# Pair 0's attention scores from fp32 row groups, with both first halves split and sent ahead, and row maxima taken for two tiles at a time

## The reference

```python
x_gate = g * jnp.tanh(jax.nn.softplus(g)); x = (x_gate * x_inner) @ W3_w.T + W3_b   # + position
h = jnp.concatenate([h, txt], axis=1)
q = (ln(h) @ Wq + bq)  # 8 heads, two halves of 16 each; k alike; v: 8 heads of 16
a1 = softmax(q1 @ k1.T * scale); a2 = softmax(q2 @ k2.T * scale)
h = h + (a1 - 0.5 * a2) @ v
h = h + experts(ln(h)) + shared(ln(h))
```

## Time and profile before

| | us |
|---|---|
| median of 3 runs | 237.06 (236.85 to 237.62) |
| the profiled execution, its own time | 235.49 |
| its span | 233.5 |
| TensorE busy | 189.9 (81%) |
| VectorE busy | 145.4 (62%) |
| ScalarE busy | 112.6 (48%) |
| GpSimd busy | 96.0 (41%) |
| first instruction of pass one of pair 0 | 33.0 |
| first instruction of pass two (start of the paired stage) | 54.2 |

### The profile page before, as it was taken

How to read it: one execution, slowest core, us unless ns; L and a number is a source line. 1 busy time by engine, 2 the same in 40 slices (tenths; PEclk the granted TensorE clock), 3 DMA queues, 4 the chain that set the end, 5 groups by cost and what they waited for, 6 DMA issues and landing times.

```text
span 233.5 us, 4897 instructions
## 1 busy us (share of the span) xinstructions
PE 189.9 (81%) x1615; PEld 135.6 (58%) x1615; DVE 145.4 (62%) x483; ACT 112.6 (48%) x213; POOL 96.0 (41%) x130
## 2 busy tenths in 40 slices
PE   0669278588988998896988999998989987999960
PEld 0538134134644554543644444468989986999950
DVE  4799779984596658798589754748333333455420
ACT  2125142033767666675477757631566645466310
POOL 4300418800882486010100006005777777777440
PEclk9999959555999999999799999999999999999996
DMA  5911986565637464859735597020444333331000
GB/s 189 297 27 50 102 152 101 110 105 102 120 91 144 98 119 57 156 103 255 253 101 179 192 273 102 0 68 3 124 103 104 87 85 80 72 64 40 25 12 0
DMA packets 20332, 25.35 MB, mean 109 GB/s; under 512 B 3393, under 2 KB 16199, under 8 KB 20308
## 3 DMA queue, kind: packets, MB, share of 16 engines
q1 hardware_dynamic: 17817, 20.68, 38.9%
q0 software_dynamic: 1888, 3.81, 7.1%
q10 hardware_dynamic: 603, 0.54, 1.6%
HBM read 12.17 MB, written 3.62 MB: 68 GB/s over the span
## 4 chain that ended last, share of the span: by engine, by line
PE 45%; DVE 19%; issue 10%; DMA 9%; POOL 6%; ACT 4%; SPq 2%; ACTq 1%; POOLq 0%; DVEq 0%
PE bank L1558 8%; PE bank L1360 7%; DVE smax L908 6%; PE bank L1313 6%; PE bank L1571 5%; PE bank L1342 4%; DMA stacks<-parts 4%; PE bank L1291 4%; POOL p_ring L556 3%; DMA p_ring<-hb_scratch,id_u 3%; PE bank L1374 3%; ACT p_ring L668 2%; PE bank L1400 2%; DMA stacks<-mx_p 2%; PE bank L1221 1%
## 5 line engine op out<-in xcount | busy, mean ns | idle before, releaser
L908 DVE TENSOR_REDUCE smax<-bank 128x2 f32<-128x384 f32 x96 | 51.2, 552 | 22.7 <-PE bank L1313 21.9
L668 ACT ACTIVATE p_ring<-bank 128x384 f32<-128x384 f32 x96 | 44.9, 494 | 31.4 <-PE bank L1342 29.9
L1313 PE MATMUL bank<-stacks 96*128 96x192 bf16 (+1 forms) x256 | 35.7, 273 | 10.3 <-DVE smax L908 5.1
L1342 PE MATMUL bank<-stacks 99*128 99x192 bf16 (+1 forms) x256 | 32.0, 253 | 3.2 <-ACT p_ring L668 2.6
L1313 PEld LDWEIGHTS bank<-stacks 96*128 96x128 bf16 (+1 forms) x256 | 15.6, 108 | 32.5 <-DVE smax L908 16.8
L1558 PE MATMUL bank<-p_ring,parts 128*128 128x128 f32 x208 | 27.2, 276 | 0.6 <-DVE p_ring L1160 0.6
L1558 PEld LDWEIGHTS bank<-p_ring,parts 128*128 128x128 f32 x208 | 25.3, 192 | 0.8 <-DVE p_ring L1160 0.8
L742 ACT ACTIVATE p_ring<-bank 128x512 f32<-128x512 f32 x19 | 11.4, 598 | 26.3 <-PE bank L1558 26.3
L573 POOL DMA_INDIRECT out_dram<-oT,out_u x19 | 19.0, 1000 | 10.9 <-DVE oT L1186 7.0
L1342 PEld LDWEIGHTS bank<-stacks 99*128 99x128 bf16 (+1 forms) x256 | 17.3, 107 | 8.3 <-ACT p_ring L668 5.5
L556 POOL DMA_INDIRECT p_ring<-hb_scratch,id_u x19 | 19.3, 1014 | 5.8 <-issue 5.2
(11 more groups left out here) (171 smaller groups left out, 319.4 us busy)
## 6 DMA issues: line engine op xcount, KB each, us to landing
stacks<-in_w_dram SPq DMA_DIRECT2D x12, 512.0 KB, 5.0
stacks<-parts SPq DMA_DIRECT2D x47, 96.0 KB, 3.6
stacks<-stacks SPq DMA_DIRECT2D x14, 192.0 KB, 3.1
stacks<-stacks SPq DMA_DIRECT2D x16, 96.0 KB, 3.5
wp_sb<-in_wpack_dram SPq DMA_DIRECT2D x1, 900.0 KB, 6.7
hb_scratch<-h SPq DMA_DIRECT2D x3, 256.0 KB, 3.0
stacks<-in_wn_dram SPq DMA_DIRECT2D x1, 512.0 KB, 4.4
hx_scratch<-hn SPq DMA_DIRECT2D x1, 387.0 KB
```

The costliest lines, as they stand in the source:

```text
L668: act.activation(p_ring[:, half % 2, TJ * (hd % 4) + ORDER[i], :, :], bank[2 + g % 2][:, 0:2 * SEQ].rearrange("p (s q) -> p s q", s=2), AC ...
L908: dve.tensor_reduce(smax[:, p % 2, j, 2 * hd:2 * hd + 2], bank[g % 2][:, 0:2 * SEQ].rearrange("p (s k) -> p s k", s=2), AX.X, ALU.max, neg ...
L1313: ins = pe.matmul(bank[g % 2][r0:r0 + rn, SEQ * s:SEQ * (s + 1)], q_st[p % NST][0:SROWS, 2 * hd + s, 128 * j + r0:128 * j + r0 + rn], k_st ...
L1342: ins = pe.matmul(bank[2 + g % 2][r0:r0 + rn, SEQ * s:SEQ * (s + 1)], k_st[p % NST][0:SROWS + NPART, 2 * hd + s, 128 * j + r0:128 * j + r0 ...
```

## The change

- Pair 0's pass one no longer uses the stacks. q and k are projected a second time with columns in another order (`rows`, L1347; weights laid out by GpSimd, eight operations), so that each group of 32 partitions holds two slots of 16. ScalarE writes them to `q_rows` and, twice, to `k_rows`, once with either slot of each group multiplied by zero (`evac_rows`). `score0(k)` then makes four matmuls in fp32, one for each group of 32 rows (eight for the middle tile), into the four banks `s_banks`. `row_max0(k)` takes four slots at once: 12 reductions of 768 columns for 24 of 384. There is one set of four banks, so `score0(k + 1)` waits for `row_max0(k)`.
- The parts of pairs 0 and 1: ScalarE makes f, hi and mid, GpSimd makes both differences (`rest`, `low`), none of it is on VectorE. The order (`TURNS0`) is first half of pair 0, first half of pair 1, second halves. Parts 4 to 7 lie in `p_ring`.
- SyncE sends in the new order below; from pair 2 on the parts of the second half's q go before the maximum and the copies of the first half. ScalarE issues no copies and no maximum any more.
- The gate matmuls of group 2 go before pair 0's turns; its gate function is shared by GpSimd (six operations) and VectorE (product and reciprocal). Pair 1's norm is made ahead of the first row maximum, that of tiles 6 to 11 between the maxima, and ScalarE normalises all six of these tiles in one go after it.

```diff
+        s_banks = ctx.enter_context(nc.psum_tensor("s_banks", [128, 4, 512], F32))
+        bank = [s_banks[:, i, :] for i in range(4)] + [ctx.enter_context(nc.psum_tensor(f"bank{i}", [128, 512], F32)) for i in range(4, 8)]
...
         GH = TJ * HEADS // 2
         p_ring = sb("p_ring", [128, 2, GH, 2, SEQ])
+        EARLY_Q = 2 * PT
+        EARLY_K = EARLY_Q + HS // 4 * PT
+        early = p_ring[:, 0, :, :, :].rearrange("p g s q -> p (g s q)")
+        q_rows = early[:, 0:EARLY_Q].rearrange("p (c t) -> p c t", c=2)
+        k_rows = early[:, EARLY_Q:EARLY_K].rearrange("p (u t) -> p u t", u=HS // 4)
+        wq_rows, wk_rows = [early[:, EARLY_K + 256 * m:EARLY_K + 256 * (m + 1)].rearrange("p (c n) -> p c n", c=2) for m in range(2)]
+        early_parts = p_ring[:, 1, :, :, :].rearrange("p g s q -> p (g s q)")[:, 0:4 * NPART * PT // 2].bitcast(BF16)\
...
+        ROWS0 = [("rows", c, m) for c in range(2) for m in range(2)]
+        misc_order = ROWS0[0:2] + proj_items(0)[0:2] + ROWS0[2:4] + proj_items(1)[0:2] + proj_items(0)[2:5] + proj_items(1)[2:4] + [("max", 0, 0), ("proj", 1, 4)]
...
                 if p >= NST:
                     sp.wait_ge(st_ready, TJ * HEADS * (p - NST + 1))
-                for m, st, order in ((0, q_st[b], Q_PARTS), (1, k_st[b], K_PARTS)):
+                todo = [(part, m) for m in ms for part in range(NPART)]
+                for part, m in sorted(todo) if p < 2 else todo:
+                    st, order = ((q_st[b], Q_PARTS), (k_st[b], K_PARTS))[m]
                     r = 4 * p + 2 * ch + m
-                    for part in range(NPART):
-                        j = order.index(part)
-                        if part < 2:
...
                     .then_inc(max_ld[p % NST][ch], 16)
-            for ch in range(2):
-                gather_parts(1, ch)
-                copy_blocks(1, ch)
+            gather_parts(0, 0)
+            gather_parts(1, 0)
+            copy_blocks(0, 0)
+            copy_blocks(1, 0)
+            gather_parts(0, 1)
+            load_max(0, 0)
+            gather_parts(1, 1)
+            copy_blocks(0, 1)
+            load_max(0, 1)
...
+            sp.wait_ge(h_mm, 3)
+            ones_rows(2)
             for p in range(2, PAIRS):
-                load_max(p - 2, 1)
                 gather_parts(p, 0)
+                gather_parts(p, 1, (0,))
+                if p == PAIRS - 1:
+                    gather_parts(p, 1, (1,))
...
+            def rest(k):
+                f = f_ring[:, k % NF, :]
+                pool.wait_ge(hi_act, k + 1)
+                pool.tensor_tensor(f, f, parts_of(TURNS0[k])[:, 0, :], ALU.subtract).then_inc(rest_done, 1)
+            def low(k):
+                pr = parts_of(TURNS0[k])
+                pool.wait_ge(rest_done, k + 1)
+                pool.wait_ge(mid_act, k + 1)
+                pool.tensor_tensor(pr[:, 2, :], f_ring[:, k % NF, :], pr[:, 1, :], ALU.subtract).then_inc(split_done[k % NF], 1)
...
+                    for l in range(2):
+                        pool.tensor_scalar(dst[:, :, l, :], src[:, :, l, :], by, 0.0, ALU.mult, ALU.add).then_inc(w_rows_done, 1)
+            last = GROUPS[2]
+            pool.wait_ge(ex_done, 3)
+            link(pool.tensor_scalar(gm[:, last], ex[:, last], 1.0, 2.0, ALU.mult, ALU.add))
+            link(pool.tensor_tensor(mu[:, last], gm[:, last], ex[:, last], ALU.mult))
+            link(pool.tensor_scalar(mu[:, last], mu[:, last], MISH_TOP, 0.0, ALU.min, ALU.add))
+            pool.tensor_scalar(mr[:, last], mu[:, last], 1.0, 2.0, ALU.mult, ALU.add).then_inc(mr_done, 1)
+            for k in range(2):
+                rest(k)
+            for k in range(2):
+                low(k)
+            pool.wait_ge(rec_done, 1)
+            link(pool.tensor_tensor(mu[:, last], mu[:, last], ex[:, last], ALU.mult))
+            pool.tensor_tensor(g_sb[:, last], mu[:, last], inner[:, last], ALU.mult).then_inc(act_done, 1)
+            pool.wait_ge(act_done, 3)
+            for k in range(2, ACT_SPLITS, 2):
+                rest(k)
+                rest(k + 1)
+                low(k)
+                low(k + 1)
+            pool.wait_ge(split_done[(ACT_SPLITS - 1) % NF], 2)
+            for r in range(ACT_SPLITS, 4 * PAIRS):
                 split(r)
...
+            def evac_rows(c, m, l=0):
+                item = ("rows", c, m)
+                act.wait_ge(misc_ready, misc_no[item] + 1)
+                src = mbank(item)[:, 0:PT]
+                if m == 0:
+                    act.activation(q_rows[:, c, :], src, ACT.Identity, bias=bqw4[:, c:c + 1]).then_inc(wide_done, 1)
+                else:
+                    act.activation(k_rows[:, 2 * c + l, :], src, ACT.Identity, bias=bkw[:, 2 * c + l:2 * c + l + 1], scale=rows_of[:, l:l + 1]).then_inc(wide_done, 1)
...
-            exp_gate(2)
-            copies_k0(True)
-            copies_k0(False)
+            act.wait_ge(bq_done, 3)
+            act.wait_ge(rows_done, 1)
+            def f_hi(k):
+                evac_proj(TURNS0[k] // 4, TURNS0[k] % 4)
+                hi(k)
+            evac_rows(0, 0)
+            evac_rows(0, 1, 0)
+            evac_rows(0, 1, 1)
+            f_hi(0)
+            f_hi(1)
+            mid(0)
+            evac_rows(1, 0)
+            mid(1)
+            evac_rows(1, 1, 0)
+            evac_rows(1, 1, 1)
             copy_hnT(1)
-            normalise(LN_TEXT, 1)
-            for n in range(4):
-                evac_proj(1, n)
+            f_hi(2)
+            f_hi(3)
+            mid(2)
+            mid(3)
+            f_hi(4)
+            f_hi(5)
...
+            def row_max0(k):
+                u, i = divmod(k, TJ)
+                dve.wait_ge(s_ready, 2 * (k + 1))
+                dve.tensor_reduce(smax[:, 0, ORDER[i], 4 * u:4 * u + 4], s_banks[:, :, 0:SEQ], AX.X, ALU.max, negate=True).then_inc(s_max, 2)
...
+            def pair1_norm():
+                n = image_tokens(1)
                 yield
                 dve.wait_ge(dve_step, n)
-                for t in LN_LAST:
-                    n = step(dve.bn_aggr(mv[:, t, :], stats[:, t, :]))
+                yield from stats_steps((4,))
+                yield from norm_steps(slice(TJ, 2 * TJ))
+                for t in LN_FIRST:
+                    yield ln_apply((t,))
+            def last_factor():
+                c = GROUPS[2]
+                dve.wait_ge(inner_done, 3)
+                n = step(dve.scalar_tensor_tensor(inner[:, c], tok_bank(2, 0), bn_[:, 0:1], inner[:, c], ALU.add, ALU.mult))
                 yield
                 dve.wait_ge(dve_step, n)
-                n = step(dve.tensor_scalar(ve[:, sl], mv[:, sl, 1], EPS, None, ALU.add))
+                dve.wait_ge(mr_done, 1)
+                yield dve.reciprocal(ex[:, c], mr[:, c]).then_inc(rec_done, 1)
...
-                    n = step(ins)
-                    yield
-                    dve.wait_ge(dve_step, n)
-                yield ln_bias(sl)
...
-                row_max(0, a // TJ, a % TJ)
-                next(splitting, None)
-                for _ in range((a >= 3) + (a >= GH + 4)):
+                yield from stats_steps((7, 10))
+                yield from norm_steps(slice(2 * TJ, T))
+                yield ln_bias(slice(2 * TJ, T))
+            for _ in pair1_norm():
+                pass
+            splitting, last_mish, rest_text, last_norm = iter(()), last_factor(), stats_steps((6, 8, 9, 11)), last_norm_steps()
+            for k in range(TJ * HEADS // 2):
+                row_max0(k)
+                if k == 0:
+                    for _ in last_mish:
+                        pass
+                for _ in range(4 if 1 <= k <= 2 else 0):
+                    next(rest_text, None)
+                if k == 3:
+                    for _ in rest_text:
+                        pass
+                if k == 6:
+                    take_v(0)
+                for _ in range(2):
...
+            def rows(c, m, tiles=range(TJ)):
+                item = ("rows", c, m)
+                if tiles[0] == 0:
+                    wait_bank(item)
+                pe.wait_ge(hnT_done, 2 if 1 in tiles else 1)
+                pe.wait_ge(w_rows_done, 8)
+                dst = mbank(item)[:, 0:PT].rearrange("p (j t) -> p j t", j=TJ)
+                src = hnT[:, 0:PT].rearrange("p (j t) -> p j t", j=TJ)
+                t = slice(tiles[0], tiles[-1] + 1, tiles[-1] - tiles[0] if len(tiles) == 2 else 1)
+                ins = pe.matmul(dst[:, t, :], (wk_rows if m else wq_rows)[:, c, :], src[:, t, :], start=True, stop=True)
+                if 1 in tiles:
+                    ins.then_inc(misc_ready, 1)
...
+            def score0(k):
+                u, i = divmod(k, TJ)
+                j = ORDER[i]
+                if k == 0:
+                    pe.wait_ge(act_done, 2)
+                    pe.wait_ge(inner_done, 3)
+                else:
+                    pe.wait_ge(s_max, 2 * k)
+                pe.wait_ge(wide_done, 3 * (u // 2) + u % 2 + 2)
+                for r0, rn, bb in batches(j):
```

(7 more changed lines are left out.)

347 lines of the change are left out of this document (153 added, 194 removed).

## The result

The changed kernel takes 247.84 us in the median of 4 runs (246.58 to 248.59); the kernel before took 237.34 on the same chip. The ratio is 1.044, with a 95% interval of 1.038 to 1.051: **slower by 4.4%**. The forecast was 243.8. The profiled execution is the longest of the four (248.59, span 246.8), that of before was the shortest of its own (span 233.5), so the two traces differ by 13.3 us where the medians differ by 10.5.

A forecast was written before the change was run, and what follows sets the result against it. Pass two's start was taken to wait for pair 1's stack, not pass one. Pass two 1.6 us later plus 5.1 in pair 0's paired stage made 6.7 on 235.49, so 242.2; with 1.57 for medians 243.8 us, range 231.5 to 250.5.

The forecast's parts named there:

- step 3: Pair 0's paired stage: two SyncE sends now stand behind a maximum, so pair 2 starts 5.1 us later.
- Step 1: Up to the first maximum: pair 1's norm meets four GpSimd differences of 0.91 us; start at 28.5 us, 24.9 without waits.
- Step 2: Pass one's twelve maxima: 19.8 us of work, 5 not hidden, 2 meeting GpSimd; pass two starts at 55.8 us.
- M: Time at which pass two starts: 54.2 us before, forecast 55.8, 1.6 us later.
- later pairs: Pair 3's copies, issued behind twelve parts instead of nine, all ready: 0 to 0.5 us, taken as 0.
- SyncE is no bound: Rival for the paired stage: the copies are hidden anyway, pass one as forecast; 238.7 us, chance 0.14.
- Row groups don't overlap: Rival for pass one: each score takes 1.3 us instead of 0.46, 11 times; 251 to 260 us, chance 0.07.
- Half clock all through: Rival for pass one: 8 us not hidden instead of 5, pass two at 60 to 63; 248 to 251 us, chance 0.12.
- The early start wins: Rival: no GpSimd waits in the norm, clock stays up, first maximum at 24.9; 236.3 or 231 us, chance 0.27.

The follow-up runs named there:

- e6_pool_late: Changed kernel with GpSimd's first two differences and lowest parts held back until pair 1's first LayerNorm tile is written; ratio 1.040 to the kernel before.
- e3_loop_order: Changed kernel with SyncE's sends for pairs 2 and 3 put back, first half copies ahead of the maximum; ratio 1.017 to the kernel before.
- e2_copy_11_first: Changed kernel with only the copies of pair 1's second half put back ahead of pair 0's second maximum; ratio 1.015 to the kernel before.
- e11_hold_ones: Changed kernel with SyncE's order put back at both places, experts' weights held behind the late maximum, rows of ones sent earlier; ratio 0.989 to the kernel before.
- e4_before_late: Kernel before, given only the change's SyncE order for pairs 2 and 3, copies behind the maximum; ratio 1.008 to the kernel before.
- e7_v_early: Changed kernel with VectorE's v sum one maximum earlier and the first split of maxima done at once; ratio 1.047 to the kernel before.

## Why the prediction was right, and where it was short

Direction and range held (231.5 to 250.5), and step 3's mechanism, copies behind maxima, is the one that the runs show. The size was short by 4.0 us in the medians, and in the profiled executions 13.3 stand against the 6.7 of the sum.

**Step 1 (first maximum at 28.5)** came at 27.10. The mechanism was there, the size not: three small operations of VectorE met a two-input operation of GpSimd and lost 0.6 us each, and one of the three normalisations took 0.90 us instead of 0.34 beside the fourth. So the count of four was right, and each lost 0.6 and not 0.91. My 24.9 without waits is some 24.6: e6_pool_late started at 25.17 with one normalisation still at 0.94 beside a held difference.

**Step 2 (M = 55.8)** came at 54.94. The product of scores took 0.61 at the full clock and 1.02 at half, so the groups overlap, as I had taken it, with 0.46. The reduction of 768 columns took 0.94 to 0.96 (0.95). From the first maximum to M it was 27.8 us (forecast 27.3). The sum had 19.8 of work, 2 for meetings with GpSimd and 5 not hidden. Up to the end of the last maximum VectorE was busy for 19.69 us, meetings included, and idle for 7.6: the meetings were smaller than I had them and the open waits larger. What the step left out is ScalarE: the second product of scores waits for its copy of the transposed tiles.

**Step 3, M to P2 (5.1 us)** was 5.13. The wait at mid-stage was to be 2.7 and was 2.70; it starts 1.6 us earlier than I had it, because pair 0's second maximum was sent at M + 5.7 and not at M + 7.3, and the landing ends as much earlier. P2 was to be at M + 26.2 and is at M + 26.25. That it is so close is luck: from the end of the first wait to pair 1's maximum in `mx_p` it was 7.1 us, where I had taken 5.6 from before. This 1.5 us of half clock the step did not have, and it made up for the 1.6.

**Step 3, "later pairs: 0 to 0.5 us"** is the step that failed. I counted twelve parts ahead of pair 3's copies against nine before (they are six, 84.61 to 88.44), saw them ready, and left out what I had just priced for pair 2: these copies also stand behind a maximum. The wait at P3 was 2.40 instead of 0.54, and e3_loop_order, which puts the order back, has no wait there.

**The clock behind a wait** was in no term. Pass two I had taken at the speed of before with waits added. From P2 to V the changed kernel lost 7.5 us, of which the longer wait at P3 explains 1.9. Filling the waits, with the copies as late as ever, took 5.9 us off M to V in the traces and some 3.4 to 6 off the time. I had weighed the clock in pass one with care and left it out in the stage where I had forecast TensorE to stand idle for 2.7 and 3 us.

**Rivals.** "SyncE is no bound" (238.7) falls with the wait of 2.70 at its forecast place and with e2_copy_11_first, where it is gone. "Row groups don't overlap" falls with the 0.61. "Half clock all through" (M at 60 to 63) was right in its time, 248, and wrong in its place: from the first maximum to the last the clock was 0.78, the mixture of the forecast, M was 54.94, and the half clock that cost the time came in pass two. "The early start wins" had its waits in the norm against it, and they came. e6_pool_late took these waits away, the first maximum came at 25.17, and M stayed. Since that run made ScalarE late instead, what this rival's early start would have given is not shown.

## What this says for the kernel, and what stays open

The change's own idea, scores without the stacks, is worth 6.5 us at the first maximum (27.10 against 33.60) and nothing at M. From the first maximum to the end of the last it now takes 27.3 us instead of 19.2: VectorE is busy for 19.7 instead of 16.8 and idle for 7.6 instead of 2.5, in twelve alternating steps on one set of banks. Its cost is in SyncE's program and the half clock behind it. With the sends moved there (copies ahead of maxima, ones into idle time, weights behind the late maximum) M to V goes from 119.6 to 108.1, against 107.0 in the kernel before. No version was shown to be faster than that one; the nearest is e11_hold_ones, 0.989 with an interval of 0.975 to 1.003, from four runs on a single chip.

Open is what sets how long the clock stays down around a wait: 6.8 us with each of the three of the changed kernel, 3.4 us with one of 3.31 in e4_before_late and one of 2.71 in e7_v_early, not at all with 1.89 and 1.82. Open is also how much the moves of pass one are worth at a clock that stays up: TensorE ran at half from 46 to 52 us in each run with them, and in the kernel before and most of the others too.

## To carry to other kernels

- A send that is moved behind a wait in a queue is to be priced at each turn of the loop, not only at the first. List for each stage what stands ahead of it in that queue and when the last of these is ready.
- A wait of TensorE has two prices, its length and the half clock that may follow. The second is measured by giving TensorE useless work in the wait; here it was some 3.4 to 6 us for three waits of 8.4.
- Putting an order right lets through what came next in the queue. Here 512 KB of weights then overtook an 18 KB transfer on which a stage waited. Look for the small urgent transfer that now starts after the large patient one.

## What the hardware showed that I had not expected

- An 18 KB transfer, issued 1.1 us after the first of five 512 KB loads, took 6.4 us to land; with the loads held back TensorE could start 3.7 us after the issue.
- One chip took 88.6 to 89.3 us behind V, where the experts' rows are gathered, and the others 72.0 to 72.4, with the same stretches up to V. A comparison of the whole time between chips would have called e11_hold_ones 6 us slower than the changed kernel.
- Filling that overshot three waits by 7.9 us made M to V only 0.5 us longer (120.1 against 119.6): behind M the clock was at 1.00 until 123 us, where that of the changed kernel was 0.80 to 0.85.
